# Band 0 of the deformable convolution spread between the steps of its offset convolution, its loads issued by GpSimd, and the snake's step offsets stored once per image

## The reference, cut to what matters

```python
x = x + L0_conv(gn(x))   # 11x11 Gaussian blur
x = x + L1_conv(gn(x))   # 3x3 convolution, used as a gate per channel
x = x + L2_conv(gn(x))   # "snake": 9 taps moved in y by learned, accumulated offsets, bilinear
x = x + L3_conv(gn(x))   # modulated deformable 3x3 convolution
```

## Time and profile before

| | us |
|---|---|
| median of 3 runs (lowest, highest) | 3009.36 (3006.67, 3010.37) |
| the profiled execution, its own time | 3010.58 |
| the profiled execution, span in the trace | 3008.7 |
| PE busy in the span | 2446.1 (81%) |
| DVE, ACT, POOL busy | 1773.9, 1529.5, 1027.2 |
| mean granted clock of TensorE | 0.903 of full speed |

### The profile page before, as it was taken

The page is one execution under the profiler, slowest core; times in us unless marked ns, Lnnn a source line. Parts: engine busy times, 40 slices in busy tenths (PEclk is TensorE's granted clock), DMA queues, the critical chain, the costliest instruction groups (busy, mean ns, idle before and its releaser), DMA issues. The chain is left out here.

```text
span 3008.7 us, 98681 instructions
## 1 busy us (share of the span) xinstructions
PE 2446.1 (81%) x44813; PEld 1582.0 (53%) x44813; DVE 1773.9 (59%) x2823; ACT 1529.5 (51%) x1757; POOL 1027.2 (34%) x740
## 2 busy tenths in 40 slices
PE   1675993739999839999999917599996589999998
PEld 1673442527777615455555515377774344555555
DVE  5895656335555475567667661455554745666764
ACT  1222554235555444567666642255555345667665
POOL 0331000035555310355555300455552204554552
PEclk7897996869999959799999958799998688999999
DMA  1677722011111122111221130111113121211221
GB/s 34 169 203 140 110 31 112 3 39 31 27 31 27 32 111 72 55 63 66 67 69 63 53 120 11 35 34 31 27 27 120 31 73 52 69 63 66 67 70 40
DMA packets 219789, 191.42 MB, mean 64 GB/s; under 512 B 77037, under 2 KB 170785, under 8 KB 218785
## 3 DMA queue, kind: packets, MB, share of 16 engines
q1 hardware_dynamic: 219360, 185.02, 22.3%
HBM read 119.96 MB, written 65.01 MB: 61 GB/s over the span
## 5 line engine op out<-in xcount | busy, mean ns | idle before, releaser
L2211 PE MATMUL dense_banks<-dense_arena,kept_spread_yx 32*128 32x512 f32 x2432 | 477.8, 665 | 16.7 <-ACT dense_arena L2284 5.0
L1499 ACT ACTIVATE snake_samp<-snake_s 128x1024 f32<-128x1024 f32 x320 | 321.0, 1023 | 301.6 <-PE snake_s L1429 301.5
L2332 DVE TENSOR_TENSOR dense_arena<-dense_banks,dense_arena 128x1024 f32<-128x1024 f32 x256 | 301.5, 1219 | 245.3 <-PE dense_banks L2211 245.3
L1562 DVE TENSOR_SCALAR snake_hat<-snake_spread 128x1024 f32<-128x1024 f32 x256 | 301.4, 1219 | 207.4 <-PE snake_spread L1407 207.4
L2284 ACT ACTIVATE dense_arena<-dense_banks 128x1024 f32<-128x1024 f32 x256 | 248.6, 1021 | 264.7 <-PE dense_banks L2211 260.2
L1429 PE MATMUL snake_s<-snake_hat,snake_xt 64*64 64x128 f32 x10240 | 338.0, 275 | 19.3 <-ACT snake_samp L1499 19.1
L2261 PEld LDWEIGHTS dense_banks<-dense_arena 64*64 64x64 f32 x11264 | 266.9, 133 | 145.3 <-ACT dense_arena L2304 94.4
L2304 ACT ACTIVATE dense_arena<-dense_banks 128x864 f32<-128x864 f32 (+1 forms) x384 | 299.2, 834 | 65.7 <-PE dense_banks L2261 65.5
L1429 PEld LDWEIGHTS snake_s<-snake_hat,snake_xt 64*64 64x64 f32 x10240 | 285.6, 134 | 85.6 <-issue 42.2
L2261 PE MATMUL dense_banks<-dense_arena 64*64 64x108 f32 x11264 | 307.8, 257 | 0.5
L2273 PE MATMUL dense_banks<-dense_arena,kept_w_dcn 64*64 64x264 f32 x4608 | 285.0, 388 | 3.6 <-ACT dense_arena L2304 3.6
(11 more groups left out here) (326 smaller groups left out, 3565.2 us busy)
## 6 DMA issues: line engine op xcount, KB each, us to landing
dense_arena<-offs SPq DMA_DIRECT2D x576, 56.0 KB
x<-blur_x SPq DMA_DIRECT2D x16, 1024.0 KB, 5.1
pre<-snake_ob SPq DMA_DIRECT2D x32, 512.0 KB, 4.0
out<-dense_arena SPq DMA_DIRECT2D x64, 256.0 KB, 3.1
gateconv_low<-x SPq DMA_DIRECT2D x24, 512.0 KB, 9.5
dense_arena<-offs SPq DMA_DIRECT2D x256, 48.0 KB
offs<-dense_arena SPq DMA_DIRECT2D x64, 144.0 KB
residual0Silu_x<-x SPq DMA_DIRECT2D x16, 512.0 KB, 10.7
```

Of the source, the lines that this page charges most:

```text
L1499: act.activation(samp[u % 2][:, :, i * MS:(i + 1) * MS, :, :].rearrange("p b m t h -> p b (m t h)"), sample_at(u, i)[:, :, :], ACT.Copy).t ...
L1562: ins = dve.tensor_scalar(strided(hat[u % 2][:, 0:1], GUARD + (4 * tau + 2 * half) * SW * SR, [[8, 2], [SW * SR, 2], [SR, SW], [1, 8]]), s ...
L2211: return pe.matmul(bank[:, :], self.k.spread_yx[r, kind, :], self.cp[u % 2][r, tile, :], start=True, stop=True)
L2332: dve.tensor_tensor(h, self.p_hat[pair][:, :, :].rearrange("p t (r x) -> p (t r) x", x=W), h, ALU.mult).then_inc(self.main_ready, 1)
```

## The change

It has three parts.

1. `steps` in DRAM takes the layout of `raw`, (128, 4, 16, 128). SP issues one transfer for each image, all 128 partitions, as soon as that image's tanh is done: 4 transfers of 1 MB instead of 16 of 144 KB. The snake's loads take the same bytes from the new places.
2. The 30 transfers that load bands 0 and 1 are issued by GpSimd, after its staging work, and wait as before for the stores of unit 0 and its means. They have semaphores of their own.
3. The work of band 0 is put between steps of the convolution. It uses `p_hat[0]` (banks 0 and 1) alone, so its four pairs go one after the other. The convolution has banks 2 to 6, and all means share bank 7, with a wait for the previous mean to be kept. ACT, DVE and PE take their parts at fixed accumulations or steps. ACT's `keep_odd` moves from after unit 2 to after unit 1, and DVE's `turn_patches` from after unit 1 to after n = 4.

```diff
-            for half in range(2):
-                sp.wait_ge(tanh_ready, 2 * half + 2)
-                of = slice(2 * half, 2 * half + 2)
-                for q in range(4):
-                    for odd in range(2):
-                        p0 = C * q + HC * odd
-                        sp.dma_start(steps[:, of, 2 * q + odd, :, :], raw[p0:p0 + Y_CH, of, :, :]).then_inc(stored, 16)
-            sp.wait_ge(stored, 16 * 16)
+            for b in range(GI):
+                sp.wait_ge(tanh_ready, b + 1)
+                sp.dma_start(steps[:, b, :, :], raw[:, b, :, :]).then_inc(stored, 16)
+            sp.wait_ge(stored, 16 * GI)
...
+    steps_v = steps.rearrange("(h c) b k w -> c b h k w", c=HC)
...
+FIRST_CLIP, SECOND_CLIP = 13, 29
+FIRST_Y, FIRST_X = (41, 46, 51, 56), (44, 49, 54, 59)
+FIRST_LAST, FIRST_MOD = 62, 65
+KEEP_Y, PRODUCT = (15, 17, 19, 21), (16, 19, 21, 23)
+KEEP_LAST, KEEP_MOD = 24, 25
...
-        conv = TileConv(... [d.arena.banks[:, i, :] for i in range(6)])
+        conv = TileConv(s, xn, k.w_off3, 6, NU, 9, lambda u, q: RU * u + q, 4, [d.arena.banks[:, i, :] for i in range(2, 7)])
-        p_mean = [d.arena.banks[:, 6 + i, :] for i in range(2)]
+        p_mean = d.arena.banks[:, 7, :]
...
             def mean(u):
                 pe.wait_ge(sig_ready, GI * (u + 1))
-                if u >= 2:
-                    pe.wait_ge(mean_kept, u - 1)
+                if u >= 1:
+                    pe.wait_ge(mean_kept, u)
...
                 if rest == 0 and 0 <= u < NU - 1:
                     mean(u)
+                if at in FIRST_Y:
+                    d.first_y(pe, FIRST_Y.index(at))
+                elif at in FIRST_X:
+                    d.first_x(pe, FIRST_X.index(at))
+                elif at == FIRST_LAST:
+                    d.first_last(pe)
+                elif at == FIRST_MOD:
+                    d.first_mod(pe)
...
-            d.spread_first(pe)
...
+                    if n in KEEP_Y:
+                        d.first_keep(act, KEEP_Y.index(n))
+                    elif n == KEEP_LAST:
+                        d.first_keep_last(act)
+                    elif n == KEEP_MOD:
+                        d.first_keep_mod(act)
...
-            d.keep_first(act)
...
             d.keep_even(pool, 0)
+            pool.wait_ge(stored[0], 64)
+            pool.wait_ge(mod_stored[0], 64)
+            d.load_first(pool)
...
+                    if n in PRODUCT:
+                        d.first_product(dve, PRODUCT.index(n))
                     x = cm[u % 2][:, b, :, :]
...
+                    if n == 4:
+                        d.turn_patches(dve, 0)
+                    elif n == FIRST_CLIP:
+                        d.clip_y(dve, 0)
+                        d.clip_x(dve, 0)
+                    elif n == KEEP_LAST:
+                        d.product_last(dve, 0)
+                    elif n == SECOND_CLIP:
+                        d.clip_y(dve, 1)
+                        d.clip_x(dve, 1)
...
-            d.products(dve, 0, 0)
-            d.products(dve, 0, 1)
-            d.product_last(dve, 0)
...
-                if u == 2:
-                    sp.wait_ge(stored[0], 64)
-                    sp.wait_ge(mod_stored[0], 64)
-                    d.load_first(sp)
...
+    def first_y(self, pe, j):
+        i, pair = divmod(j, 2)
+        if j == 0:
+            pe.wait_ge(self.y_clipped, 1)
+        else:
+            pe.wait_ge(self.main_ready, j)
+        for at in range(2):
+            ins = self.spread(pe, self.p_hat[0][:, at, :], 0, 2 * pair + at, 2, 1 + i)
+        ins.then_inc(self.y_spread, 1)
...
+    def first_product(self, dve, j):
+        dve.wait_ge(self.x_spread, j + 1)
+        t = 4 * (j // 2) + 2 * (j % 2)
+        h = self.hat[0][:, t:t + 2, :, 0:W].rearrange("p t r x -> p (t r) x")
+        dve.tensor_tensor(h, self.p_hat[0][:, :, :].rearrange("p t (r x) -> p (t r) x", x=W), h, ALU.mult).then_inc(self.main_ready, 1)
```

More of the change, by code:

```diff
@@ L1265 @@
 NM = SU // 2
-Y_CH = 9
 GUARD = 8 * SR
@@ L1932, in _ @@
             pe.wait_ge(far_ready, 1)
-            pe.wait_ge(mean_kept, NU - 1)
-            pe.matmul(p_mean[NU % 2][0:1, 0:P], far1[:, :], k.ident, start=True, stop=True).then_inc(far_turned, 1)
-            d.spread_first(pe)
+            pe.wait_ge(mean_kept, NU)
+            pe.matmul(p_mean[0:1, 0:P], far1[:, :], k.ident, start=True, stop=True).then_inc(far_turned, 1)
         @block.scalar
@@ L1942, in keep_mean @@
                     act.wait_ge(mod_stored[u % 2], u // 2 * 64)
-                act.activation(mm[u % 2][:, :, :].rearrange("p i w -> p (i w)"), p_mean[u % 2][:, :], ACT.Copy).then_inc(mean_kept, 1)
+                act.activation(mm[u % 2][:, :, :].rearrange("p i w -> p (i w)"), p_mean[:, :], ACT.Copy).then_inc(mean_kept, 1)
             for u in range(NU):
@@ L2129, in __init__ @@
         self.ones_set = s.sem("ones_set")
+        self.first_loaded = [s.sem(f"first_loaded{i}") for i in range(2)]
         self.loaded = [s.sem(f"loaded{i}") for i in range(2)]
@@ L2161, in load @@
     def load(self, sp, u):
+        done = self.first_loaded[u] if u < 2 else self.loaded[u % 2]
         def put(tile, block_, ch, times):
@@ L2164, in put @@
             sp.dma_start(self.cp[u % 2][32 * block_:32 * block_ + GI * times, tile, :],
-                         bass.AP(tensor=at.tensor, offset=at.offset, ap=[[H * W, GI], [0, times], [1, 4 * W]])).then_inc(self.loaded[u % 2], 16)
+                         bass.AP(tensor=at.tensor, offset=at.offset, ap=[[H * W, GI], [0, times], [1, 4 * W]])).then_inc(done, 16)
         for i in range(4):
@@ L2170, in load @@
                          bass.AP(tensor=y.tensor, offset=y.offset, ap=[[H * W, 2 * GI], [0, 3], [1, 4 * W]])
-                         ).then_inc(self.loaded[u % 2], 16)
+                         ).then_inc(done, 16)
         for tile in range(2):
@@ L2176, in load @@
         put(3, 1, K2 - 1, 3)
-        sp.dma_start(self.cp[u % 2][64:64 + GI, 3, :], self.offs[MOD, :, 4 * u:4 * u + 4, :].rearrange("b h w -> b (h w)")).then_inc(self.loaded[u % 2], 16)
+        sp.dma_start(self.cp[u % 2][64:64 + GI, 3, :], self.offs[MOD, :, 4 * u:4 * u + 4, :].rearrange("b h w -> b (h w)")).then_inc(done, 16)
     def stage(self, pool, u):
@@ new lines, in first_y, with first_x @@
+    def first_y(self, pe, j):
+        i, pair = divmod(j, 2)
+        if j == 0:
+            pe.wait_ge(self.y_clipped, 1)
+        else:
+            pe.wait_ge(self.main_ready, j)
+        for at in range(2):
+            ins = self.spread(pe, self.p_hat[0][:, at, :], 0, 2 * pair + at, 2, 1 + i)
+        ins.then_inc(self.y_spread, 1)
+    def first_x(self, pe, j):
+        i, pair = divmod(j, 2)
+        if j == 0:
+            pe.wait_ge(self.x_clipped, 1)
+        pe.wait_ge(self.y_kept, j + 1)
+        for at in range(2):
+            ins = self.spread(pe, self.p_hat[0][:, at, :], 0, 2 * pair + at, i, 0)
+        ins.then_inc(self.x_spread, 1)
@@ new lines, in first_last, with first_mod, first_keep @@
+    def first_last(self, pe):
+        pe.wait_ge(self.main_ready, 4)
+        self.spread(pe, self.p_hat[0][:, 1, :], 0, 1, 3, 1)
+        self.spread(pe, self.p_hat[0][:, 0, :], 0, 0, 3, 0).then_inc(self.last_spread, 1)
+    def first_mod(self, pe):
+        pe.wait_ge(self.hat_ready, 1)
+        self.spread(pe, self.p_hat[0][:, 0, :], 0, 2, 3, 3).then_inc(self.mod_spread, 1)
+    def first_keep(self, act, j):
+        act.wait_ge(self.y_spread, j + 1)
+        t = 4 * (j // 2) + 2 * (j % 2)
+        act.activation(self.hat[0][:, t:t + 2, :, 0:W].rearrange("p t r x -> p (t r) x"),
+                       self.p_hat[0][:, :, :].rearrange("p t (r x) -> p (t r) x", x=W), ACT.Copy).then_inc(self.y_kept, 1)
@@ L2480, in build @@
     by_row = nc.dram_tensor("by_row", (H, W, OFFS), F32).ap()
-    steps = [nc.dram_tensor(f"steps{g}", (Y_CH, GI, 8, H // 8, W), F32).ap() for g in range(NG)]
+    steps = [nc.dram_tensor(f"steps{g}", (P, GI, H // 8, W), F32).ap() for g in range(NG)]
     table = nc.dram_tensor("table", (GI * PX, C), F32).ap()
```

48 lines of the change are left out of this document (19 added, 29 removed).

## The result

The kernel after the change takes 2979.95 us (median of 4, 2975.93 to 2981.25), the kernel before on the same chip 3008.02 (3003.30 to 3010.37). The ratio is 0.9907, 95% interval 0.9892 to 0.9922: faster by 28 us. I had forecast 2988 in a range of 2963 to 3008. The sum was 8 us off, but it is made of terms of which four were off by 2 to 14 us, in opposite directions.

A forecast was written before the change was run, and what follows sets the result against it. PE was taken to bound dcn_offsets, busy 116.2 of 128.5 us. The terms -20.0 - 17.8 + 18.0 + 22.2 - 24.2 = -21.8 us took the profiled 3010.6 to 2988.8, median 2988 us; range 2963 to 3008.

The forecast's parts named there:

- pause removed: In dcn_offsets' convolution, the gap at unit 5 goes once the loads leave SP's queue: -20.0 us.
- tail: End of dcn_offsets: the dense run starts 8.9 us earlier a group, with SP's mean stores the next limit: -17.8 us.
- ten pieces: Band 0's spread calls and mean, put into PE's convolution, lengthen it by 9.0 us a group: +18.0 us.
- wait for the loads, and the clock behind it: PE idles 7.9 us for the clipped y after step 41, plus 3.2 at half clock, each group: +22.2 us.
- five banks, one mean bank: In dcn_offsets' convolution, five accumulation banks instead of six leave a slack of 0.8 us and cost nothing.
- step offsets: End of snake_offsets: full-width stores at 350 GB/s land at 624.4 instead of 636.5, 12.1 us a group: -24.2 us.
- the likeliest case: The forecast itself: GpSimd takes 0.85 to 1.3 us per load issue, giving 2988 us; chance 0.44.
- the prediction's own signs: Wrong if PE's step 41 wait is under 3 or over 16 us, issues far from 1 us, or ACT releases PE's first taps.
- c = 1.02: Time in us for GpSimd to issue one load, taken from its iota; PE then idles 7.9 us.
- 15c - 7.4: PE's idle time in us at step 41, waiting for band 0's 15 loads, with c us per GpSimd issue.
- rival A: GpSimd issues loads as fast as SP, so the idle term falls from 22.2 to 4.7 or less: 2970 us; chance 0.25.
- I take 0.9: Cost in us of each piece put into PE's convolution, near the upper end of 0.5 to 1.0.

The follow-up runs named there:

- Part 2 alone: The kernel before with only the loads of bands 0 and 1 moved to GpSimd, ahead of its keep_even: 2988.53 us, ratio 0.9932.
- parts 1 and 2 together: The kernel before with the new step stores and the loads on GpSimd, without the spreading of band 0: 2961.17 us, ratio 0.9845.
- the run with doubled calls: All band 0 pieces one unit later than in the changed kernel, both spread calls of each y and x piece issued twice: 2983.65 us, ratio 0.9916.
- The run with 16 partitions: The kernel before with the new step layout, stored in sixteen transfers of 16 neighbouring partitions and two images each: 3008.63 us, ratio 1.0004.
- its best form here: Changed kernel with all band 0 pieces one unit later: 2971.29 us; also both clips early, last mean stores on GpSimd and ScalarE: 2969.40 us.

## Why the prediction was right in sign and near in size

Both groups together, in us; "measured" is read from the traces.

| term | predicted | measured |
|---|---|---|
| pause removed | -20.0 | -20.0 (gap gone) |
| tail | -17.8 | -16.0 |
| ten pieces | +18.0 | +23.4 |
| wait for the loads, and the clock behind it | +22.2 | +8.7 |
| five banks, one mean bank | 0 | 0 in the steady part |
| step offsets | -24.2 | -28.3 |
| sum | -21.8 | -32.2 (spans: -31.1, medians: -28.1) |

**The pause: right.** Part 2 alone shows it. Its cause, the loads in front of unit 3's store in SP's queue, was read correctly from the earlier trace rows.

**The size: near, and in part by luck.** The two errors on the gaining side, 13.5 us too much for the wait and 4.1 too little for the step offsets, were in part made up by 5.4 too little for the pieces and 1.8 too much for the tail.

**The loads on GpSimd: mis-sized, and the likeliest case was not the one that came.** By the prediction's own signs (a wait under 3 us, issues far from 1 us) its deciding term was wrong: the wait is 2.0 us and an issue 0.60. The step that failed is "c = 1.02", taken from the iota as the nearest row. The issue takes 0.60 us, below even the 0.65 of SP that I had set as the lower bound. With c = 0.60 my own formula gives 15c - 7.4 = 1.6 us of idle time, and 2.1 with the landing of 2.5 us instead of 2.0; it was 2.00. So the formula was right and the duration in it wrong: this is rival A, with a chance of 0.25. But rival A was mis-sized as well, since I gave it no clock loss, and its 2970 missed by 10 us where the forecast missed by 8. A wait of 2 us cost 3.1 us of lowered clock in group 0 and 1.6 in group 1, half to all of what the long pause had cost. A's +4.7 should have been +8.7 or more.

The warning that I had quoted from the Trainium skill (SBUF: State Buffer), that GpSimd's descriptors are held up by DVE, did not decide anything here. Ten issues take 6.01 us in the kernel after and in parts 1 and 2 together, with DVE at reductions and additions beside them. The one clearly longer case is the loads of band 1 in group 0 of the kernel after, 6.50 us with DVE's clip beside it; in group 1, with the same clip, it is 6.04. Whether those 0.5 us are what the Trainium skill warns of is not shown, and no run tries a DVE mode in which they would be more.

**The pieces: mis-sized.** "I take 0.9" was reasoned from the call's own length and from a share that could run beside it. A piece costs 1.17: 0.86 for the calls and 0.3 beside them, by the run with doubled calls. By the stretched units nothing of it ran beside the convolution.

**The tail: nearly right.** 14.1 us for 13.3; SP's stores are the next limit, as said. The last placing on DVE came 0.6 us late behind the second clip, which I had not counted.

**The step offsets: mis-sized, on the good side.** I took 350 GB/s between 290 and 410; it is 425. I read the earlier trace rows as half the engines only, and noted 235 GB/s at full share as a bound. The run with 16 partitions shows that this bound is what a small, narrow transfer really does (242). The estimate by engines alone from the Trainium skill (DMA: Bandwidth & Descriptors, Why a DMA increments its semaphore by 16 and not by 1), 200 GB/s, comes near that run (193) and not the change.

**Five banks: right for this kernel, and for a narrower reason than given.** With five banks the means stay 10.73 us apart in the steady part, so the slack was enough there. Before the pause was removed the sixth bank hid 2.3 us of it; I had not asked what a bank is worth at a stall.

**What I did not ask.** The sum of parts 2 and 3 was +2.4 in my own working, with -20.0 of it owed to part 2. By that, part 3 cost 22.4 us (-17.8 + 18.0 + 22.2), and I did not say that the change without it would be better. The runs show 19 us against it as built and 8 to 10 in its best form here. The reason stands in the columns of the earlier trace rows: PE, on which the pieces were put, was the bound of that block (116.2 of 128.5 us), so they cost their full length there.

## What to carry to other kernels

Before moving work off a tail into a loop, ask whether the engine that gets it is idle there: here 11.7 us of pieces on the busiest engine bought 8.0 us of tail. Loads queued ahead of a store that another engine waits for cost 10 us a group here, and another engine's queue, which was free, was the cheap cure. Storing over all 128 partitions in one transfer of 1 MB paid even with 1.8 times the bytes. Place the first dependent matmul late enough that TensorE doesn't wait, as a wait of 2 us cost up to 5.

## What was not expected of the hardware

- GpSimd issues a load of offsets in 0.60 us and SyncE in 0.65; ScalarE issues a mean store in 1.13, SyncE in 0.79.
- TensorE's granted clock fell from 1.00 to 0.50 after a wait of 2.00 us, and the next 96 matmuls took 5.71 us for 3.44; in group 1, after 1.96 us, they took 4.87.
- At a DMA share of 1.00 to 1.02 the rate was 197 GB/s with 256 KB in 16 partitions a transfer and 425 with 1024 KB in 128: a full share is not a full rate.
